# Attention probabilities left unnormalised, outputs multiplied by the reciprocal row sums on GpSimd

## The reference, cut to what matters

```python
xn = layernorm(x)                                 # x: 4 x 512 x 1024
qkv = xn @ w_qkv                                  # 32 query heads, 8 key/value heads, D = 128
scores = einsum('bqhgd,bkhd->bhgqk', q, k) * D ** -0.5
bias = -slopes * sqrt(maximum(rel, 0))            # -inf where the key is later than the query
attn = softmax(scores + bias, axis=-1)
out = einsum('bhgqk,bkhd->bqhgd', attn, v) @ w_o
return x + out + ffn(xn)                          # ffn: a dense layer and a routed low-rank one
```

## Time and profile before

| what | us |
|---|---|
| median of 3 runs | 2512.18 (2511.98 to 2513.4) |
| the profiled execution | 2510.83 |
| its span, first to last instruction | 2508.5 |
| PE busy | 2413.6 |
| DVE busy | 1503.8 |
| ACT busy | 1382.8 |
| POOL busy | 779.4 |
| mean granted clock of TensorE | 0.986 |

### The profile page before, as it was taken

How to read it: one execution, slowest core, us unless ns; L and a number is a source line. 1 busy time by engine, 2 the same in 40 slices (tenths; PEclk the granted TensorE clock), 3 DMA queues, 4 the chain that set the end, 5 groups by cost and what they waited for, 6 DMA issues and landing times.

```text
span 2508.5 us, 35023 instructions
## 1 busy us (share of the span) xinstructions
PE 2413.6 (96%) x12128; PEld 2049.7 (82%) x12128; DVE 1503.8 (60%) x2817; ACT 1382.8 (55%) x3075; POOL 779.4 (31%) x1029
## 2 busy tenths in 40 slices
PE   5999999997899999999799999999999999999999
PEld 4787888886778888888688888888888888888887
DVE  6657455565755555545566666666656666666664
ACT  4432133334534123333777777777777777777764
POOL 3211000000320100000334535446345364454634
PEclk8999999998999999999999999999999999999999
DMA  4536344545345544543755565655656556555543
GB/s 148 189 132 213 134 161 158 201 174 218 115 135 185 176 151 168 201 169 141 279 193 188 184 214 182 219 175 182 220 188 218 185 183 212 195 201 201 185 168 126
DMA packets 118319, 455.93 MB, mean 182 GB/s; under 512 B 11945, under 2 KB 12089, under 8 KB 109184
## 3 DMA queue, kind: packets, MB, share of 16 engines
q1 hardware_dynamic: 86176, 334.37, 38.6%
q0 software_dynamic: 31968, 119.33, 13.7%
HBM read 276.96 MB, written 176.69 MB: 181 GB/s over the span
## 4 chain that ended last, share of the span: by engine, by line
PE 87%; ACT 5%; DVE 4%; DMA 2%; issue 1%; POOL 1%; SPq 0%; DVEq 0%; ACTq 0%; POOLq 0%
PE ps L637 27%; PE ps L639 27%; PE ps L638 27%; PE ps L824 5%; ACT wo L886 1%; ACT probs L1026 1%; DVE stats L1135 1%; ACT pt_hi L886 1%; DMA q<-qk_s 1%; ACT rows L915 1%; ACT probs L1040 1%; DVE w_lo L1121 0%; ACT res_hi L886 0%; DMA lora_lo<-lora_s 0%; DVE pt_lo L1121 0%
## 5 line engine op out<-in xcount | busy, mean ns | idle before, releaser
L886 ACT ACTIVATE w_hi<-raw 128x1024 fp32r<-128x1024 f32 x196 | 207.0, 1059 | 559.3 <-PE ps L639 440.3
L1121 DVE TENSOR_TENSOR w_lo<-raw,w_hi 128x1024 fp32r<-128x1024 f32 x196 | 239.1, 1224 | 357.8 <-ACT w_hi L886 357.6
L1389 DVE TENSOR_TENSOR acc<-ps,acc 128x512 f32<-128x512 f32 x448 | 298.3, 687 | 249.5 <-issue 225.1
L637 PE MATMUL ps<-x_hi,w_hi 128*128 128x512 f32 x1120 | 436.2, 389 | 0.0
L639 PE MATMUL ps<-x_hi,w_lo 128*128 128x512 f32 x1120 | 435.8, 389 | 0.0
L638 PE MATMUL ps<-x_lo,w_hi 128*128 128x512 f32 x1120 | 435.7, 389 | 0.0
L637 PE MATMUL ps<-wo,op_hi 128*128 128x512 f32 x896 | 365.5, 408 | 24.1 <-DVE wo L1121 24.1
L1026 ACT ACTIVATE probs<-probs,neg_max 128x512 f32<-128x512 f32 (+3 forms) x512 | 284.2, 567 | 172.2 <-DVE neg_max L1358 172.2
L639 PE MATMUL ps<-wo,op_lo 128*128 128x512 f32 x896 | 355.3, 397 | 0.0
L638 PE MATMUL ps<-wo,op_hi 128*128 128x512 f32 x896 | 354.4, 396 | 0.0
L1358 DVE CUSTOM_DVE_ANT_0 probs<-ps,bias 128x512 f32<-128x512 f32 (+3 forms) x512 | 220.7, 487 | 111.4 <-PE ps L639 107.5
(11 more groups left out here) (155 smaller groups left out, 4700.6 us busy)
## 6 DMA issues: line engine op xcount, KB each, us to landing
raw<-w_all SPq DMA_DIRECT2D x70, 1024.0 KB, 5.3
q<-qk_s SPq DMA_DIRECT2D x128, 512.0 KB, 3.9
acc<-acc_s SPq DMA_DIRECT2D x128, 512.0 KB, 5.2
acc_s<-acc SPq DMA_DIRECT2D x112, 512.0 KB, 7.8
qk_s<-res_hi POOLq DMA_DIRECT2D x40, 1024.0 KB, 4.6
qk_s<-res_a POOLq DMA_DIRECT2D x20, 1024.0 KB, 9.1
qk_s<-res_b POOLq DMA_DIRECT2D x20, 1024.0 KB, 5.2
k<-qk_s SPq DMA_DIRECT2D x32, 512.0 KB, 3.6
```

Source lines behind the costliest of these rows:

```text
L637: pe.matmul(to, st_hi, mv_hi, start=start, stop=False, skip_group_check=True)
L886: nc.scalar.activation(to, source, ACT.Copy).then_inc(signal, 1)
L1121: nc.vector.tensor_tensor(to, source, high.bitcast(F32), ALU.subtract).then_inc(signal, 1)
L1389: nc.vector.tensor_tensor(to, fill[f % 2][:, :], to, ALU.add).then_inc(s_acc, 1)
```

## The change

The probabilities are not multiplied by the inverses any more; PE transposes them as soon as the exponentials are there. ACT copies the output as before and signals `s_at_copy`. SP writes the inverses of a unit (128 partitions by 4, the queries of the four blocks) to DRAM, waits for the landing, and reads them back as 512 numbers on each of the 128 partitions (`spread`). GpSimd multiplies the output by them in place (`scaled`), at the start of its iteration n for unit n-2, with the inverses read with a step of four numbers, and this now signals `s_at_raw`, for which the sums and highs of the set wait. Of the seven steps of `w_o`, the high of step 4 moves from ahead of the exponentials to the end of the iteration in front, its low from DVE to the end of GpSimd's iteration (`out_split`), and the low of step 6 takes its place on DVE; PE, SP and `wo_sums` wait for step 4 by a semaphore of its own (`low_made`). Some small tiles move to make room; the cut diff leaves those out.

```diff
-HIGHS_FIRST = {10: (4, 6)}
-HIGHS_LAST = {8: (0, 1), 9: (3, 2), 10: (5,)}
+HIGHS_FIRST = {10: (6,)}
+HIGHS_LAST = {8: (0, 1), 9: (3, 2, 4), 10: (5,)}
 LOWS_EARLY = {9: (0,), 10: (2,)}
-LOWS_MIDDLE = {9: (1,), 10: (4,)}
-LOWS_LAST = {9: (3,), 10: (6, 5)}
+LOWS_MIDDLE = {9: (1,), 10: (6,)}
+LOWS_LAST = {9: (3,), 10: (5,)}
+
+BY_DVE = (0, 1, 3, 2, 6, 5)
+LOWS_POOL = {10: (4,)}
+BY_POOL = (4,)
...
-        row_inv = at("row_inv", rest + 1632, [P, QT])
+        row_inv = at("row_inv", rest + 704, [P, 2, QT])
...
+        inv_all = [at("inv_all0", 54 * K, [P, P * QT]), at("inv_all1", rest + 736, [P, P * QT])]
...
+        inv_s = nc.dram_tensor("inv_s", (2, P * QT), F32).ap()
...
+            def spread(n):
+
+                if not 0 <= n < UNITS:
+                    return
+                sp.wait_ge(s_inv, n + 1)
+                if n >= 2:
+                    sp.wait_ge(s_at_raw, n - 1)
+                sp.dma_start(inv_s[n % 2].rearrange("(p i) -> p i", i=QT), row_inv[:, n % 2, :]).then_inc(s_inv_s, 16)
+                sp.wait_ge(s_inv_s, 16 * (n + 1))
+                if n == 0:
+                    sp.wait_ge(s_bank, 4 * TOTAL)
+                sp.dma_start(inv_all[n % 2][:, :], inv_s[n % 2].partition_broadcast(P)).then_inc(s_inv_all[n % 2], 16)
...
+                spread(n - 2)
                 out_weights(n)
                 sums_in_and_out(n)
             for n in range(UNITS, UNITS + 3 * G):
+                spread(n - 2)
                 sums_in_and_out(n)
...
+            def out_split(group, step):
+
+                pool.wait_ge(s_wo_hi, made(group, step))
+                for i in range(4):
+                    cut = slice(i * 256, (i + 1) * 256)
+                    last = nc.gpsimd.tensor_tensor(wo[:, step, 1, cut], wo_source(step)[:, cut],
+                                                   wo[:, step, 0, cut].bitcast(F32), ALU.subtract)
+                last.then_inc(s_wo_low, 1)
+
+            def scaled(n):
+
+                pool.wait_ge(s_at_copy, n + 1)
+                pool.wait_ge(s_inv_all[n % 2], 16 * (n // 2 + 1))
+                tile = at_raw[n // G % 2][n % G // 2][:, n % 2, :].rearrange("p (i q) -> p i q", i=QT)
+                nc.gpsimd.tensor_tensor(tile, tile, inv_all[n % 2][:, :].rearrange("p (q i) -> p i q", i=QT),
+                                        ALU.mult).then_inc(s_at_raw, 1)
+
             for n in range(UNITS + G + 2):
                 s, new_sums, new = shaped(n)
+                if 2 <= n < UNITS + 2:
+                    scaled(n - 2)
                 if new_sums:
                     pool.wait_ge(s_at_raw, G * (s + 1))
...
+                for group, step in making(n, LOWS_POOL):
+                    out_split(group, step)
...
             def transposes(n):
-                pe.wait_ge(s_probs, n + 1)
+                pe.wait_ge(s_exp, QT * (n + 1))
...
-                        pe.wait_ge(s_at_raw, n)
+                        pe.wait_ge(s_at_copy, n)
...
                 act.wait_ge(s_neg_max, QT * n + c + 1)
+                if n and c == 0:
+                    act.wait_ge(s_inv, n)
...
-                high(at_raw[s % 2][n % G // 2][:, n % 2, :], ps_o[:, :], s_at_raw)
-
-            def normalise(n):
-                act.wait_ge(s_inv, n + 1)
-                for i in range(QT):
-                    tile = probs[:, n % 2, OFF[i]:OFF[i] + (i + 1) * P]
-                    last = nc.scalar.activation(tile, tile, ACT.Copy, scale=row_inv[:, i:i + 1])
-                last.then_inc(s_probs, 1)
+                high(at_raw[s % 2][n % G // 2][:, n % 2, :], ps_o[:, :], s_at_copy)
...
-                if n < UNITS:
-                    normalise(n)
...
             def inverses(n):
                 dve.wait_ge(s_exp, QT * (n + 1))
-                if n:
-                    dve.wait_ge(s_probs, n)
-                nc.vector.reciprocal(row_inv[:, :], row_sum[:, :]).then_inc(s_inv, 1)
+                if n >= 2:
+                    dve.wait_ge(s_inv_s, 16 * (n - 1))
+                nc.vector.reciprocal(row_inv[:, n % 2, :], row_sum[:, :]).then_inc(s_inv, 1)
```

More of the change, by code:

```diff
@@ L111, in block_program @@
         ident = at("ident", rest, [P, P])
[L112 to L123, removed]
-        row_inv = at("row_inv", rest + 1632, [P, QT])
+        slopes = at("slopes", rest + 512, [P, HEADS])
+        neg_max = at("neg_max", rest + 640, [P, QT])
+        row_sum = at("row_sum", rest + 672, [P, QT])
+        row_inv = at("row_inv", rest + 704, [P, 2, QT])
+        stats = at("stats", rest + 736, [P, 2, 2, 6])
+        moments = at("moments", rest + 864, [P, TT, 2])
+        rstd = at("rstd", rest + 928, [P, TT])
+        root = at("root", rest + 960, [P, TT])
+        newton = at("newton", rest + 992, [P, TT])
+        shift = at("shift", rest + 1024, [P, TT])
+        gbias = at("gbias", rest + 1056, [P, E])
+        gate_buf = at("gate_buf", rest + 1088, [P, 2, TT, E])
+        gate_col = at("gate_col", rest + 1344, [P, 10, TT])
         d_mask = at("d_mask", rest + 1664, [P, QT, R])
@@ L216, in block_program @@
         s_wo_lo = sem("s_wo_lo")
+        s_wo_low = sem("s_wo_low")
         s_bias = sem("s_bias")
@@ L221, in block_program @@
         s_inv = sem("s_inv")
-        s_probs = sem("s_probs")
+        s_inv_s = sem("s_inv_s")
+        s_inv_all = [sem(f"s_inv_all{i}") for i in range(2)]
         s_pt = sem("s_pt")
@@ L226, in block_program @@
         s_o = sem("s_o")
+        s_at_copy = sem("s_at_copy")
         s_at_raw = sem("s_at_raw")
@@ L342, in made, with low_made @@
             return STEPS * group + WO_ORDER.index(step) + 1
+        def low_made(group, step):
+            if step in BY_POOL:
+                return s_wo_low, len(BY_POOL) * group + BY_POOL.index(step) + 1
+            return s_wo_lo, len(BY_DVE) * group + BY_DVE.index(step) + 1
         def used(group, step):
@@ L423, in out_weights @@
                 if n % GROUP_UNITS == 2 * G + 2 and group + 1 < GROUPS:
-                    sp.wait_ge(s_wo_lo, STEPS * (group + 1))
+                    sp.wait_ge(s_wo_lo, len(BY_DVE) * (group + 1))
+                    sp.wait_ge(s_wo_low, len(BY_POOL) * (group + 1))
                     sp.wait_ge(s_wo_sum, len(WO_SUMS) * (group + 1))
@@ L615, in wo_sums @@
                 if step == 5:
-                    pool.wait_ge(s_wo_lo, made(group, 1))
+                    pool.wait_ge(*low_made(group, 1))
                 for i in range(4):
@@ L844, in fill_in @@
                 if s % (SETS // GROUPS) == 0 and tile == 0:
-                    pe.wait_ge(s_wo_lo, made(s // (SETS // GROUPS), k))
+                    pe.wait_ge(*low_made(s // (SETS // GROUPS), k))
                 pe.wait_ge(s_op_lo, f + 1)
```

## The result

| | before | after |
|---|---|---|
| median | 2512.53 us (2511.98 to 2513.4, 4 runs) | 2540.34 us (2539.58 to 2540.86, 4 runs) |
| profiled execution, span | 2510.83, 2508.5 us | 2540.86, 2539.1 us |

The ratio is 1.0109, with a 95% interval of 1.0096 to 1.0122: slower by 27.8 us where 7 were forecast. The sign held and the size was four times the forecast. The stated range, 2498 to 2541, held by 0.7 us and by luck: its upper end was put there for a slow strided read, which the trace rules out, and the forecast's own range, 2513 to 2528, was missed. From the page of the changed kernel, against the earlier trace rows: busy times, then the group of the product (mean 1560 ns), then DMA issues with the median time to landing.

What follows compares the result with a forecast made beforehand. PE's own work was taken to bound the stage, other engines counting only at 8 turns and both ends. Turns 6.0, start 1 and end 0.2 make 7 us more: 2518 for the profiled execution, 2519 as median, range 2498 to 2541.

Steps and rivals of the forecast that it cites:

- the forecast's own range: Range of the main case, GpSimd's queue making step 4 late at the turn: 2513 to 2528 us, chance 0.52.
- What bounds the kernel: PE's own work bounds the stage; other engines matter only at the 8 turns and the stage's two ends.
- Normalise removed, hidden in 127 of 128 units: ACT's four activations, 1.8 us a unit, are hidden by PE's work; only the first unit's wait, 1.6 us, counts.
- The product's price, 1.6 us: GpSimd's added 128x512 product per unit takes 1.6 us, with ends of 1.28 and 2.82.
- far-slower rival: GpSimd's strided read makes the product 2.82 us; 30 us more in all, 2542 us; chance 0.13.
- First consequence: At a turn, the product delays the highs by 1.6 us against 1.8 removed: the chain to step 2 gains 0.2 us.
- a second piece of the wait: At a turn, up to 1.5 us of PE's wait moves ahead of the transposes, behind the low of part 0.
- Second consequence: At a turn, GpSimd's queue of 22.3 us makes step 4 ready 0.75 us late; eight turns, 6.0 us.
- the prediction's own sign: At the turns: the prediction is wrong if step 4 never makes PE wait.
- The start, +1: At the stage's start, SP's store and broadcast delay q by 2.5 us, against 1.6 of normalise saved: 1 us more.
- The end, +0.2: At the stage's end, the last set's part 0 comes 1.6 us later: 0.2 us more, up to 1.4.
- Faster through the clock: At the turns, the split wait keeps PE's full clock: 1.7 us a turn, 14 us in all, 2498 us; chance 0.25.

Runs made afterwards that it cites:

- with q mended: Changed kernel with SP's spread split: a unit's inverses stored at the end of an iteration, broadcast in the next behind its q; 2538.70 us.
- the new order on the changed kernel: Changed kernel with split spread, earlier weight sum of step 5, all w_o lows on DVE, late highs, step 2 ahead of step 3; 2524.35 us, ratio 1.0048.
- the best kernel: Kernel before the change with later highs of steps 4 and 6, earlier weight sum of step 5, step 2 ahead of step 3; 2492.19 us, ratio 0.9917.

## Why the prediction was right in sign and wrong in size

- **What bounds the kernel:** right. All units between turns are unchanged to 0.0 us, with the product and without `normalise`.
- **Normalise removed, hidden in 127 of 128 units:** right for the time between turns. Without the product, the removal and the move of step 4 together gain 7.3 us at the turns; what the removal alone is worth there is not shown.
- **The product's price, 1.6 us:** right in size (1.56) and by luck: I took it from a contiguous row with DVE working beside it, but without the step this product takes 1.29 us, so the rest is the step's. The far-slower rival (2.82) fell, and yet its total of 2542 was nearest.
- **First consequence, 0.2 us gained a turn. This is the step that failed; that the turn's loss sits in GpSimd's queue was right.** I followed the chain through ACT alone, and there it was about right: with the weight sum out of the way the wait is 2.75 us, a gain of 0.36. I hadn't read that the low of step 2 also waits for GpSimd's weight sum of step 5, which had 1.34 us to spare before. With that sum late, and the low then held up by the product that starts in front of it, each wait grew by 1.13 us. The later turns took 2.4 us each, 16.6 in all, the half clock included. Nor was there a second piece of the wait ahead of the transposes: PE's line for `op_lo` is absent, and all that shows there is 0.17 us of issue.
- **Second consequence, step 4 late by 0.75 us, 6 us in all:** not seen, and by the prediction's own sign that made it wrong. The queue's 22.3 us were right (22.1), but PE came later than forecast, and step 4 had been done for 1 us. It is real behind the first, 1.2 to 2.5 us once the sum is moved. The move as a whole had the wrong sign: put back, step 4 costs 8.1 us.
- **The start, +1:** mis-sized. I put the store at 4 us; it took 6 to 9 in the first units, and the cover of 20 us for q wasn't there for four loads. A second road was overlooked: with q mended, the inverses of the first set hold up its outputs. Start and first turn measured 12.4 us, some 2 of which belong to the first turn's own wait, by the 2.4 us that a later turn costs.
- **The end, +0.2:** +0.4.
- **Faster through the clock:** the mechanism exists, but this change never reached it. The waits of 1.44 us kept the full clock at all seven later turns, those of 2.33 to 2.36 lost it at four or five of seven, those of 3.11 and 4.24 at all seven. Length is not all: with the new order on the changed kernel the clock over the unit was 0.88 at two of the seven turns and 1.00 at five, with the same wait of 1.8 us.

What stays open: in the changed kernel the later turns vary between 1.6 and 2.9 us with the same wait of 4.24, by how long the half clock lasts; what sets that I haven't shown. What the removal of `normalise` is worth without the move of step 4 was not run. Nor did I try the inverses on another queue.

## What to carry to other kernels

Before an instruction is put in front of another engine's queue, read in the code every semaphore wait of the instruction on the critical wait, not only the one that the trace names: those that were met in time leave no row, and the slack of each (here 1.34 us) is the price limit for the new work. Work moved from an engine with slack on average can still land in the one stretch where the receiving engine sets the end, and there the order in the queue was worth more than the work: 20.7 us gained by a new order, 27.8 lost by the change. A small round trip through DRAM was priced here by what stood behind it in its queue, not by its bytes: with SP's waiting taken off the front of q, as many bytes moved and the start's loss was gone.

## What the hardware showed that I had not expected

- A store of 2 KB, 16 bytes from each partition, took 5.0 us in the median of 128, and 8.93 and 8.16 at the start, behind 512 KB loads.
- A DVE subtraction and a GpSimd product, both with two inputs in SBUF, met at the two places shown, and the one that started 0.15 or 0.33 us behind was longer by most of the other (2.45 for 1.21 us on DVE; 2.53 for 1.56 on GpSimd). The Trainium skill says this of the port pair that both share (SBUF — State Buffer, SBUF: two separate sides), that whichever starts first has it for the whole instruction, and it counts a DVE operation with two SBUF inputs beside a GpSimd one that reads SBUF; the rows agree: the low ended 1.08 us after the product's end.
- A read with a step of 16 bytes cost GpSimd's product 21%.
- A wait shorter by 1.4 us gave 2.5 us a turn, as the granted clock then stayed at its upper level of 2.4 GHz; seven such turns were 17.6 of the 18.2 us by which the best kernel's span is shorter.
